# Layer 3's cross-attention: ScalarE exponentials per head from the scores, rounding shared with GpSimd

## The reference

```python
B, N, M, D, H = (2, 512, 77, 128, 16)       # as it is called here
DH = D // H; SCALE = DH ** (-0.5)

def _fq(x, delta, zp, n_bits):
    xi = round(x / delta) + zp
    xq = clip(xi, 0.0, 2.0 ** n_bits - 1.0)
    return (xq - zp) * delta

def _attn(x, ctx, wq, wk, wv, wo, bo, dq, dk, dv, dw):
    q, k, v = heads(x @ wq), heads(ctx @ wk), heads(ctx @ wv)
    sim = einsum('bhid,bhjd->bhij', _fq(q, dq, 128.0, 8), _fq(k, dk, 128.0, 8)) * SCALE
    attn = softmax(sim, axis=-1)
    out = einsum('bhij,bhjd->bhid', _fq(attn, dw, 0.0, 8), _fq(v, dv, 128.0, 8))
    return merged(out) @ wo + bo

x = _attn(h1, h1, a1_wq, ...) + x           # layer 3, self-attention ("L3.sa")
h2 = _ln(x, ln2_g, ln2_b)
x = _attn(h2, context, a2_wq, ...) + x      # layer 3, cross-attention ("L3.ca"): the change
h3 = _ln(x, ln3_g, ln3_b)                   # then the gated feed-forward, and the end
```

## Time and profile before

| | us |
|---|---|
| three runs | 578.42, 579.68, 579.95 (median 579.68) |
| the profiled execution | 578.32 |
| its span | 576.6 |
| mean granted TensorE clock, as a share of full speed | 0.748 |
| last instruction of the self-attention's rounding on POOL | ends at 490.1 |
| cross-attention's first maxima on DVE | start at 488.6 |
| last `keys` of the cross-attention on DVE | start at 546.13 |
| feed-forward's first matmul | starts at 550.58 |

### The profile page before, as it was taken

How to read it: one execution, slowest core, us unless ns; L and a number is a source line. 1 busy time by engine, 2 the same in 40 slices (tenths; PEclk the granted TensorE clock), 3 DMA queues, 4 the chain that set the end, 5 groups by cost and what they waited for, 6 DMA issues and landing times.

```text
span 576.6 us, 7976 instructions
## 1 busy us (share of the span) xinstructions
PE 410.9 (71%) x2721; PEld 215.6 (37%) x2721; DVE 367.9 (64%) x808; ACT 247.1 (43%) x481; POOL 238.3 (41%) x378
## 2 busy tenths in 40 slices
PE   6769665966888999966897597266666656344497
PEld 3535544633333433333522455022223222222346
DVE  2543656254999511145833516999998898989742
ACT  2003332313100466632073151789997786334341
POOL 4024033255300244434000122599997799236420
PEclk9758965978899999997598689555555555655699
DMA  9300000000000000000000000278886668122401
GB/s 273 117 1 1 3 1 1 1 0 0 1 2 1 1 1 2 1 1 1 0 1 0 2 0 2 41 141 148 147 154 119 115 123 149 37 47 51 86 1 36
DMA packets 88974, 26.08 MB, mean 45 GB/s; under 512 B 81061, under 2 KB 88167, under 8 KB 88935
## 3 DMA queue, kind: packets, MB, share of 16 engines
q1 hardware_dynamic: 88935, 25.58, 22.5%
HBM read 5.61 MB, written 0.52 MB: 11 GB/s over the span
## 4 chain that ended last, share of the span: by engine, by line
PE 40%; DVE 32%; POOL 19%; issue 5%; ACT 2%; DMA 2%; POOLq 0%; DVEq 0%; ACTq 0%
POOL k_stack L554 12%; DVE k_stack L1616 8%; PE ps L785 6%; PE ps L799 5%; POOL stats L545 3%; PE ps L677 3%; PE ps L618 3%; PE ps L689 3%; DVE stats L1710 2%; DVE xh L1291 2%; POOL rstd L467 2%; PE ps L808 2%; PE ps L610 2%; DVE cr_max L1401 2%; DVE cr_sum L1415 2%
## 5 line engine op out<-in xcount | busy, mean ns | idle before, releaser
L1710 DVE TENSOR_REDUCE stats<-ps 128x2 f32<-128x1024 f32 x64 | 77.7, 1214 | 2.4 <-PE ps L1045 2.0
L1148 ACT ACTIVATE e_buf<-ps 128x1024 f32<-128x1024 f32 (+4 forms) x56 | 39.6, 778 | 86.2 <-PE ps L785 86.2
L1247 ACT ACTIVATE e_buf<-ps,stats,sders 128x512 f32<-128x512 f32 x88 | 67.7, 774 | 18.3 <-POOL stats L545 18.3
L1065 PE MATMUL ps<-k_stack,q_stack 128*32 128x128 bf16 x512 | 38.6, 307 | 40.7 <-DVE k_stack L1723 40.6
L554 POOL TENSOR_SCALAR k_stack<-e_buf,stats 128x512 int16<-128x512 f32 x88 | 62.7, 723 | 2.1 <-DVE stats L1717 1.5
L465 POOL TENSOR_SCALAR rstd<-mv 128x4 f32<-128x4 f32 x18 | 4.1, 228 | 140.2 <-DVE mv L1285 137.2
L1065 PEld LDWEIGHTS ps<-k_stack,q_stack 128*32 128x32 bf16 x512 | 22.3, 129 | 70.3 <-DVE k_stack L1723 68.3
L1616 DVE TENSOR_REDUCE k_stack<-ps 128x4 f32<-128x1024 f32 (+3 forms) x32 | 45.0, 1483 | 2.6 <-PE ps L758 2.6
L1045 PE MATMUL ps<-q_stack 32*128 32x512 bf16 x128 | 37.6, 588 | 12.4 <-ACT e_buf L1247 8.9
L413 POOL TENSOR_SCALAR_AFFINE_SELECT e_buf<-e_buf 128x256 f32<-128x256 f32 x44 | 17.6, 407 | 66.1 <-ACT e_buf L1148 65.3
L610 PE MATMUL ps<-ident,xh 128*128 128x128 f32 x80 | 18.9, 383 | 33.6 <-DVE xh L1291 32.6
(11 more groups left out here) (269 smaller groups left out, 881.5 us busy)
## 6 DMA issues: line engine op xcount, KB each, us to landing
wsq<-in_squares SPq DMA_DIRECT2D x3, 384.0 KB, 4.7
k_stack<-k_stack SPq DMA_TRANSPOSE x64, 3.1
spread<-in_spread SPq DMA_DIRECT2D x1, 896.0 KB, 6.7
x<-in_x SPq DMA_DIRECT2D x1, 512.0 KB, 4.2
l_w<-in_L_xattn_W_ff SPq DMA_DIRECT2D x2, 256.0 KB, 7.1
l_w<-in_L_xattn_fc_w SPq DMA_DIRECT2D x2, 256.0 KB, 7.7
l_w<-in_L_xattn_ff_w SPq DMA_DIRECT2D x1, 512.0 KB, 8.7
out<-x SPq DMA_DIRECT2D x2, 256.0 KB, 2.3
```

The costliest lines, as they stand in the source:

```text
L1065: mm = pe.matmul(ps[BAND * band:BAND * (band + 1), 7, qb * P:(qb + 1) * P], v_band[:, kb, b, V * band + v, :], t_keys[n % len(t_keys)][:, ...
L1148: act.activation(e_ring[n % len(e_ring)][0:rows, :, 0:N - kb * P], ps[0:rows, 2 * (n % 3):2 * (n % 3) + 2, 0:N - kb * P], ACT.Exp).then_in ...
L1247: act.activation(e_ring[n % len(e_ring)][:, j, :], ps[:, 2 * (n % 3) + j, :], ACT.Exp, bias=stats[:, 1, c:c + 1], scale=sders[:, 8:9], acc ...
L1710: dve.tensor_reduce(stats[:, 0, c:c + 2], ps[:, 2 * (n % 3):2 * (n % 3) + 2, :], AX, ALU.max, negate=True).then_inc(S("ints.nm"), 1)
```

## The change

- DVE no longer writes the shifted scores. `maxima(i)` writes the negated maxima (signal `cross.nm`) and `shifted` is gone.
- POOL multiplies the negated maxima by the score's scale, `sders[:, 9:10]`, into a new tile `cr_shift` (`flat_shifts(i)`, signal `cross.m`), one tile ahead of its other work.
- ACT takes the exponentials from PSUM, head by head: 16 instructions of 77 columns, each with a column of `cr_shift` as bias and `sders` as scale, both [128, 1] operands in SBUF. PE may overwrite the banks once they are done (`cross.exp`).
- The rounding is parted: ACT takes the first 770 columns (FLAT_FRONT, 10 heads), POOL the other 462 behind its multiplication (signal `cross.tail`). The DMA waits for both; POOL waits for the DMA that has read the buffer two tiles before, and ACT's exponentials wait for both parts of the tile that had the buffer.

```diff
+FLAT_FRONT = 10 * M
@@ SP
                     sp.wait_ge(S("cross.rounded"), i + 1)
+                    sp.wait_ge(S("cross.tail"), i + 1)
@@ GpSimd
-            def flat_scaled():
-
+            def flat_shifts(i):
+                pool.wait_ge(S("cross.nm"), i + 1)
+                pool.tensor_scalar(cr_shift[:, i % 4, :], cr_max[:, i % 4, :], sders[:, 9:10], None, ALU.mult
+                                   ).then_inc(S("cross.m"), 1)
+
+            def flat_rounded():
+
+                flat_shifts(0)
                 for i in range(T):
                     if i == 1:
                         rstds_of("L3.ln2", 1)
                     if i == 5:
                         for h in range(B):
                             add_bias("L3.co", "L3.ln2.xh", h, B)
-                    e = flat_e[i % len(flat_e)].rearrange("p (h m) -> p h m", m=M)
+                    if i + 1 < T:
+                        flat_shifts(i + 1)
+                    e = flat_e[i % len(flat_e)]
+                    by_head = e.rearrange("p (h m) -> p h m", m=M)
                     pool.wait_ge(S("cross.recip"), i + 1)
-                    pool.tensor_tensor(e, e, cr_rec[:, i % 4, :].unsqueeze(2).broadcast_to([P, H, M]), ALU.mult
-                                       ).then_inc(S("cross.scaled"), 1)
+                    pool.tensor_tensor(by_head, by_head, cr_rec[:, i % 4, :].unsqueeze(2).broadcast_to([P, H, M]),
+                                       ALU.mult).then_inc(S("cross.scaled"), 1)
+                    if i >= len(flat_rows):
+                        pool.wait_ge(*turned(PAIRS + i - len(flat_rows)))
+                    pool.wait_ge(S("cross.scaled"), i + 1)
+                    pool.tensor_scalar(flat_rows[i % len(flat_rows)][:, FLAT_FRONT:FLAT], e[:, FLAT_FRONT:FLAT], 1.0, 0.0,
+                                       ALU.mult, ALU.add).then_inc(S("cross.tail"), 1)
@@ TensorE
-                        pe.wait_ge(S("cross.sub"), i - 1)
+                        pe.wait_ge(S("cross.exp"), i - 1)
@@ ScalarE
+                def exps(i):
+                    act.wait_ge(S("cross.m"), i + 1)
+                    if i >= len(flat_e):
+                        act.wait_ge(S("cross.rounded"), i - len(flat_e) + 1)
+                        act.wait_ge(S("cross.tail"), i - len(flat_e) + 1)
+                    for g, (h0, n) in enumerate(CROSS_GROUPS):
+                        for h in range(h0, h0 + n):
+                            ins = act.activation(flat_e[i % len(flat_e)][:, h * M:(h + 1) * M],
+                                                 ps[:, 3 * (i % 2) + g, (h - h0) * M:(h - h0 + 1) * M], ACT.Exp,
+                                                 bias=cr_shift[:, i % 4, h:h + 1], scale=sders[:, 9:10])
+                    ins.then_inc(S("cross.exp"), 1)
...
-                    act.activation(flat_rows[i % len(flat_rows)][:, 0:FLAT], flat_e[i % len(flat_e)], ACT.Identity
-                                   ).then_inc(S("cross.rounded"), 1)
+                    act.activation(flat_rows[i % len(flat_rows)][:, 0:FLAT_FRONT], flat_e[i % len(flat_e)][:, 0:FLAT_FRONT],
+                                   ACT.Identity).then_inc(S("cross.rounded"), 1)
...
-                        act.wait_ge(S("cross.sub"), i + 1)
-                        e = flat_e[i % len(flat_e)]
-                        act.activation(e, e, ACT.Exp, scale=sders[:, 9:10]).then_inc(S("cross.exp"), 1)
+                        exps(i)
@@ VectorE
-                        ins = dve.tensor_reduce(m[:, h0:h0 + n], s, AX, ALU.max)
-                    then(ins)
-
-                def shifted(i):
-                    m = cr_max[:, i % 4, :]
-                    if i >= len(flat_e):
-                        dve.wait_ge(S("cross.rounded"), i - len(flat_e) + 1)
-                    for s, (h0, n) in zip(banks_of(i), CROSS_GROUPS):
-                        ins = dve.tensor_tensor(by_head(flat_e[i % len(flat_e)][:, h0 * M:(h0 + n) * M]), s,
-                                                m[:, h0:h0 + n].unsqueeze(2).broadcast_to([P, n, M]), ALU.subtract)
-                    ins.then_inc(S("cross.sub"), 1)
+                        ins = dve.tensor_reduce(m[:, h0:h0 + n], s, AX, ALU.max, negate=True)
+                    ins.then_inc(S("cross.nm"), 1)
```

More of the change, by code:

```diff
@@ L149, in build @@
                                      pt=PAIRS, pv=PAIRS)),
-            "cross": (["L3.ca"], dict(s=T, sub=T, exp=T, recip=T, scaled=T, rounded=T, keys=T, pv=T, q=B)),
+            "cross": (["L3.ca"], dict(s=T, nm=T, m=T, exp=T, recip=T, scaled=T, rounded=T, tail=T,
+                                       keys=T, pv=T, q=B)),
             "ff": (["L1.ff", "L2.ff", "L3.ff"], dict(h=B * FC, hid=B * FC)),
@@ L1434, in rest @@
                             maxima(i)
-                            shifted(i)
                         if i == 2:
@@ L1447, in rest @@
                     normal("L3.ln3", 0)
-                return maxima, shifted, recips, rest
+                return maxima, recips, rest
             dve.wait_ge(S("const.made"), 7)
@@ L1724, in keys @@
                                       ).then_inc(S("ints.pt"), 1)
-                cross_maxima, shifted, cross_recips, rest = cross()
+                cross_maxima, cross_recips, rest = cross()
                 for n in range(PAIRS + KEYS_BEHIND):
```

8 lines of the change are left out of this document (3 added, 5 removed).

## The result

The changed kernel takes 584.52 us (median of nine runs, 581.90 to 586.65). The kernel before, in nine runs of its own, takes 579.74 (578.14 to 580.48). The ratio is 1.0087, with a 95% interval from 1.0063 to 1.0111: **slower by 0.9%**. The profiled execution took 586.43 us, with a span of 584.7.

A forecast was written before the change was run, and what follows sets the result against it. VectorE bounds the late cross-attention tiles at 5.26 us; ScalarE would bound them at 5.85. `keys(7)` 3.8 us later on the profiled 578.32 gives 582.1, for a median 583.5 us; range 577.0 to 588.0.

The forecast's parts named there:

- The bound moves to ScalarE: Late cross-attention tiles: ScalarE's exponentials and rounding take 5.85 us a tile, above VectorE's 5.26 before.
- The second operand: Exponentials by head: the scale operand beside the bias adds 0.087 us to each, making one 0.414 us.
- The second ring: DMA landing, `keys`, maxima, shift, exponentials, rounding: 11.8 us for two tiles, 5.9 each, no cost beyond ScalarE's but no slack.
- POOL's queue: At i = 5 the shift of tile 6 stands behind two `add_bias` (2.5 us), so ScalarE waits 1.3 us.
- The first four tiles: Tiles 0 to 3: VectorE's saving is lost to longer exponentials before `state_out`; second batch's queries ready at 514.3, about as before.
- The way out: From the end of exponentials(7) to the start of `keys(7)`: 8.35 us, where 10.25 stood.
- From the profiled execution to the median: The runs' median was 1.36 us above the profiled execution, so 582.1 became a median of 583.5 us.
- The clock at the end: TensorE's rise to full clock at the feed-forward may shift up to 2 us against the work: about 1 us either way.
- Hidden operands: Rival: operand reading hidden in a row of equal exponentials, 0.23 us between starts, `keys(7)` 3.4 us earlier, 576.3 us; chance 0.16.
- Partly hidden: Rival: exponentials 0.27 to 0.30 us from start to start, -0.5 to +2 us, 580.5 us; chance 0.17.
- No overlap: Rival: short exponentials do not overlap, 0.414 us from start to start, some 12 us more, 592 us; chance 0.03.
- A slipping ring: Rival: `keys` land amid POOL's multiplication and take 1.41 us instead of 0.49; +2.5 us, 586 us; chance 0.17.

The follow-up runs named there:

- keys_later_adds_late: Changed kernel with `keys` four and outputs five tiles behind (instead of three and four) and POOL's two `add_bias` at i = 7: 582.22 us, ratio 1.0041.
- adds_late: Changed kernel with POOL's two `add_bias` at i = 7 instead of i = 5: 585.23 us, ratio 1.0092 to the kernel before.
- before_again: The kernel before, unchanged, measured and profiled once more: 580.27 us, ratio 1.0014.
- no_scale_operand: Changed kernel with the exponentials' scale as an immediate number instead of an operand in SBUF: 579.69 us, ratio 1.0009 to the kernel before.
- six_heads_biases_early: six_heads_dve_shift with POOL's two `add_bias` at i = 3 instead of i = 7: 575.50 us, ratio 0.9944 to the kernel before.
- after_again: The changed kernel, unedited, measured and profiled once more: 585.20 us, ratio 1.0107 to the kernel before.
- six_heads_kept: keys_later_adds_late with six heads made the old way (VectorE subtracts, one exponential of 462 columns), ten from PSUM: 578.56 us, ratio 0.9990 to the kernel before.
- six_heads_dve_shift: six_heads_kept with the shift (maxima times scale) on VectorE right behind the maxima instead of on POOL: 578.21 us, ratio 0.9987 to the kernel before.
- rounding_parted_only: The kernel before with only the rounding parted (ScalarE 770 columns, POOL 462), subtractions and exponentials as before: 580.93 us, ratio 1.0021.

## Why the prediction was right, step by step

The time was forecast at 583.5 us and slower; it is 584.52. The stage was to be 3.8 us longer and is 4.95. Point by point, with the prediction's own steps:

- **The bound moves to ScalarE, 5.85 us a tile:** right, 5.83, but two terms in it were off and cancel, which is luck. The spacing was 0.319 and is 0.300, so the rounding starts 4.82 us behind the first exponential, not 5.11. The rounding was to hold up the next instruction for 0.74 and holds it up for 1.01. Of this 0.10 is its length, 0.94 instead of 0.84: it starts while the last exponential is still under way, and that one runs long. The rest is an overlap that isn't there. Exponentials(i) wait for the rounding that last read their buffer, and by the order of the loop that is the instruction just ahead of them: they start 0.07 us after it ends (525.72 + 0.94, 526.73). Exponentials(3), which stand behind `state_out`, on which they don't wait, start 0.21 before that ends (511.12, 511.33):

```profile
510.46 0.87 ACT L1125 ACTIVATE xT<-ps,cols 128x512 f32<-128x512 f32 x1
511.12 5.12 ACT L1178 ACTIVATE qk<-ps,cr_shift,sders 128x77 f32<-128x77 f32 x16
```

So about 0.28 us of each 5.83, an estimate from these rows, are ScalarE's wait for itself, in `keys_later_adds_late` too; no run has taken it away.

- **The second operand, 0.087 us:** 0.091, by taking it away.
- **The second ring, 5.9, without slack:** right in length, as the 6.0 of `adds_late` show. In after it does not show, since the wait before tile 6 leaves it 1.1 us of room at tile 7; `keys` stretched once (0.95 us, as POOL multiplied beside it) and the tiles did not slip.
- **POOL's queue, 1.3 us:** 1.56 is the whole wait, 7.31 - 5.83 = 1.48 its cost. Moving the biases away brings back only 0.56, as the ring stands right behind them and they get in the way at the other place.
- **The first four tiles:** exponentials(0) 490.7 to 495.7, `outputs_out(1)` at 495.54, maxima(2) at 500.42, exponentials(2) 502.5 to 507.5, rounding(0) ended 508.26, all within 0.2 us on the clock of before. Then the step that failed: **3.4 us for the DMA of `keys(0)`.** It was the landing of the last transposition, and the first took 4.8. Since the middle step of the queries was quick (0.43, one of the two ends that were given), of 1.35 us late 0.87 stayed: the queries were ready at 515.17, not 514.3. Hand-overs and maxima add 0.13; exponentials(4) start 1.0 late.
- **The way out, 8.35:** 8.60. The sum took 0.7 for the last rounding, POOL's part, where ScalarE's 0.85 is the longer.
- **Together:** +1.0 at exponentials(4), 23.98 instead of 24.11 to the end of exponentials(7), -0.13, and +0.25 on the way out: 1.12 of the 1.13 that the stage is over the forecast (4.95 and 3.82).
- **From the profiled execution to the median:** 1.36 us were added, for the profiled execution of before lay below its runs. That of after took 586.43, 1.9 above its median. The sum for it, 582.1, is 4.3 off; 2.4 of this lie ahead of the stage, 0.75 behind it and 1.15 in it. The medians differ by 4.78, close to the stage's 4.95.
- **The clock at the end** was given about 1 us either way, and the 0.75 behind the stage are this term. The feed-forward's first matmul starts 4.45 us behind the last `keys` in both kernels. The 2 us from it on, before and after:

```profile
550.58:552.58 2.00, 2.00 (x6) 0.95 (x6) 1.73 (x8) 0.44 (x2) 0.00 (x0) 1.00 0.00 0
557.92:559.92 2.00, 2.00 (x4) 0.87 (x4) 1.69 (x7) 0.36 (x1) 0.00 (x0) 0.61 0.00 0
```

The clock was full from the first matmul on in before; in after it rose about 1.6 us behind it. It is not the change's: `before_again` had 0.50 in its first 2 us and 31.6 us behind the stage.

- **The rivals.** Hidden operands: fell, 0.300 stands above 0.26. It was also priced too high. `no_scale_operand` has starts 0.208 apart, closer than the 0.23 that the rival wanted, and its stage wins 1.15 us over before, not 3.4: the shift behind POOL's biases and the first landing hold it. Partly hidden, 0.27 to 0.30: the measured spacing is its upper end, for which it gave +2 us. That is what the forecast's own sum gives for it, with six rows of exponentials on the path (tiles 0, 2 and 4 to 7): 3.8 - 6 x 15 x 0.019 = 2.1. So by the spacing this rival's edge came in, and by the time the forecast: what lies between the two is mostly ScalarE's rounding and its wait for it, then the landing and the way out, which neither had. No overlap: not seen. A slipping ring: not in after, and by 0.25 us twice in `adds_late`.

The fetch that goes with the long landing can be seen in the view of DMAs. From 510 to 516 us of after, then from 504 to 509 of `six_heads_biases_early`, queues and the one issue:

```profile
q1 hardware_dynamic: 1312, 0.33, 58.1%
q8 instruction: 1, 0.02, 1.0%
issues: line engine op xcount, KB each, median us to landing
q_stack<-q_stack SPq DMA_TRANSPOSE x1, 4.8
```

```profile
q1 hardware_dynamic: 1312, 0.33, 34.2%
issues: line engine op xcount, KB each, median us to landing
q_stack<-q_stack SPq DMA_TRANSPOSE x1, 3.4
```

In after, in before (5.0 us, hidden there) and in the nine other kernels without the six heads, a packet of 0.02 MB of instructions lies in the first transposition, and it lands in 4.8 to 5.1; `after_again` has 4.9, as was expected. In the three kernels with six heads the same transposition, over the same bytes, meets none and lands in 3.4. There the packet falls into the second transposition, which lands in 3.6 to 4.0. Smaller packets, of 0.01 MB, lie in later ones, as in the third of after, which lands in 3.6, and in the third of `six_heads_kept`, which lands in 3.4. So the first of its kind is not slow in itself; a fetch goes with a delay of anything from nothing to 1.7 us, and what makes it large or small is open. No run moved the fetch alone.

## What to carry to other kernels

A pass taken off the bounding engine pays only down to the next engine's work: write the moved work out as count by spacing of the instruction that it becomes, with each operand per partition priced (0.09 us here, sixteen times a tile), before it is moved whole. Where both forms have a bound of their own, deal the items out between them until the engines' shares are level, and then look again at each queue: the place of a filler such as `add_bias` that was right in one balance cost 2.2 us in the next. A wait whose length is read from one row may have been hidden elsewhere at another length, so read every row of its kind, hidden ones too. And a semaphore between two instructions of one engine takes away the overlap that two rows without one show: here about 0.28 us a tile.

## What the runs showed of the hardware

- In a row of sixteen equal exponentials with two operands per partition the starts lie 0.300 us apart while, from the second on, each lasts longer than the one before, 0.407 to 0.498 us; with one operand 0.208 apart and 0.320 to 0.435. The mean length in a table of groups (476 ns) is therefore neither the cost of one nor the length of one alone. What stands behind such a row ends late too: 0.94 us for 770 columns, 0.85 behind an idle engine.
- A DMA transposition of 1280 columns lands in 3.4 us. With a fetch of instructions in it the first one of the stage landed in 4.8 to 5.1, in all eleven kernels that had it there; others landed in 3.4 to 4.0 with one in them, and in 3.6 (`no_scale_operand`) and 4.3 (`six_heads_dve_shift`) with two.
- Between executions of the same code the granted clock of TensorE was 0.50 to 0.79 from 20 to 24 us and 0.63 to 0.76 from 312 to 340 us, and what followed stood up to 4.6 us apart (first maxima at 486.73 and 491.35). Two profiled executions are compared by the length of a stage, not by their spans.
- VectorE's `keys` took 0.43 to 0.49 us alone, 0.95 in after beside POOL's multiplication and 2.08 in `rounding_parted_only`; a multiplication of 128x16 grew from 0.17 to 0.47 and 0.88 us beside POOL's `add_bias`.
